# Second layer of both expert layers as one fp32 product instead of three fp16 products

## The chip, the cores and the metric

The kernel runs on one NeuronCore of a Trainium2 chip. The metric is the device time of one execution in microseconds, the median of several runs.

## What is computed

A block of a network on x of shape (8, 32, 32, 96), in fp32: a mixture of 8 experts on group-normalised x, causal attention with 6 heads on layer-normalised tokens, and a mixture of 4 experts on layer-normalised tokens, each added to its input. Both expert layers have the same form. Every token goes through every expert, and the gates of all but the top two are zero:

```python
# first expert layer: E = 8, HID = 384, 96 inputs, 96 outputs
h = jnp.einsum('bhwd,edf->bhwef', x, W1) + b1
h = jax.nn.gelu(h, approximate=False)
y = jnp.einsum('bhwef,efo->bhweo', h, W2) + b2
out = jnp.einsum('bhweo,bhwe->bhwo', y, gates)
...
# second expert layer: 4 experts of the same sizes
h = jax.nn.gelu(jnp.einsum('bsd,edh->ebsh', x, w1) + b1[:, None, None, :], approximate=False)
y = jnp.einsum('ebsh,ehd->ebsd', h, w2) + b2[:, None, None, :]
out = jnp.einsum('bse,ebsd->bsd', masked, y)
```

## The kernel before

The work is one image of 1024 tokens at a time, in 8 token tiles of 128 and 2 chunks of 512. The unit of expert work is a group, one expert on one chunk: 16 groups of the first expert layer (A) and 8 of the second (C) for each image, 192 in all. A group has two halves, and TensorE works on the first layer of one group beside the second layer of the group before:

- First layer (`first_layer`, L696): for each of 3 pieces j of 128 hidden units, three fp16 products (high and low parts of weights and inputs) with 512 columns into one of two PSUM banks `ps_u`.
- Gelu (ScalarE, `moes`, L923): the same bank is read twice, once for `hid` in fp32 (L933) and once for `hidh` in fp16 (L934).
- Low part (GpSimd, L628): `hidl` = `hid` - `hidh`, in fp16.
- Second layer (`second_layer`, L706): for each of 4 token tiles i, nine products into `ps_y`: `hidh` with the high and the low part of the second weight, then `hidl` with the high part. Tokens are the stationary operand (128x128), the 96 outputs move.
- Combination (VectorE, `combine`, L1097): `ps_y` times the gate, added to `acc`, four instructions of 128x96.

The second weights are split into `w2s` (high, low, both scaled by 64) by VectorE in the chore `split_w2`, six times, during the first image. The gates carry the factor 1/64 by a factor `WS` in `normalise` (L1082), and `gates_out` (L1092) takes it off again for the bias.

Each group has 4 slots. Everything else (maxima of the attention scores, normalisations, routing, projection) is a chore with a place in a slot, written out by hand in `schedule` (L193); each engine runs through the same list of slots in program order and waits on semaphores. A steady stage is the 16 groups A of one image, with the 72 maxima of the image before, and then the 8 groups C of the image before that. Behind it stands a softmax stage (24 steps, TensorE and ScalarE), in which no expert work is done. The images 3 to 6 are a hardware loop, the others are written out. The last 16 groups C form a tail.

`project` (L845) is a chore that the change leaves alone: 8 fp32 products for each chunk, stationary `yt` 96x128, moving `wp` 96x96.

The matmuls are all recorded at L647, a helper. `hidh` and `hidl` have two buffers each, `hid` has one. ScalarE waits before it writes `hid` until GpSimd has read it (`hl_ready`).

Of the kernel before, what the change touches and what calls it, by code (L numbers as in the profile page):

```python
# [17 lines left out]
F32 = mybir.dt.float32  # L18
F16 = mybir.dt.float16
# [7 lines left out]
P = 128  # L27
# [83 lines left out]
def spread(n, slots):  # L111
# [43 lines left out]
    "split_w2":     (None, 0),  # L155
# [37 lines left out]
def schedule(it):  # L193

    if isinstance(it, int) and it == 0:
        first = [(0, "split_w2", 0), (1, "route_a", 0, 0), (1, "route_a", 1, 0), (1, "route_a", 2, 0),
                 (2, "split_w1", 1), (3, "gates_a", 0, 0), (4, "bias_a", 0, 0), (5, "bias_a", 1, 0),
                 (6, "split_w2", 1), (7, "x_load", 0)]
        first += [(8 + 2 * n, ("split_w1", "split_w2")[n % 2], 2 + n // 2) for n in range(2 * W1_PARTS - 4)]
# [96 lines left out]
def build(nc, x, cWg, cbg, cW1, cb1, cW2, cb2, w_attn, b_attn, w_proj, b_proj,  # L296
          fWg, fbg, fW1, fb1, fW2, fb2, out):
    nc.disable_value_cache = True
    with ExitStack() as ctx:
# [9 lines left out]
        w2s = sb("w2s", [P, NE * HT, 2, D], F16)  # L309
# [34 lines left out]
        hid = sb("hid", [P, HT, CH])  # L344
        hidh = sb("hidh", [P, 2, HT, CH], F16)
        hidl = sb("hidl", [P, 2, HT, CH], F16)
# [48 lines left out]
        with nc.sbuf_tensor("w1_raw", [ONE + 1, NE * HID], F32) as w1_raw, \  # L395
                nc.sbuf_tensor("w2_raw", [P, NE * HT, D], F32) as w2_raw:
            pass
# [36 lines left out]
        w2_ready = sem("w2_ready")  # L434
# [3 lines left out]
        hl_ready = sem("hl_ready")  # L438
# [33 lines left out]
        def _(sp):  # L472
# [14 lines left out]
            def load_w2(part):  # L487
                e = 2 * part
                w, e0 = (cW2, e) if e < EA else (fW2, e - EA)
                sp.dma_start(w2_raw[:, e * HT:(e + 2) * HT, :], w[e0:e0 + 2].rearrange("e (j p) o -> p (e j) o", p=P)  # L490
                             ).then_inc(w2_loaded[part], 16)
# [75 lines left out]
        def _(pool):  # L567
# [51 lines left out]
            grp = Count(GA + GC)  # L619

            def iteration(it, moe_a, attend, moe_c):
                for up, _, phase, slots in rounds(moe_a, moe_c):
                    for slot in slots:
                        j = slot % TC
                        if up and j < HT:

                            pool.wait_ge(h_ready, grp.value(HT, j + 1))
                            g.tensor_tensor(hidl[:, grp.k % 2, j, :], hid[:, j, :], hidh[:, grp.k % 2, j, :],  # L628
                                            ALU.subtract).then_inc(hl_ready, 1)
                        for name, k, b in chores(it, phase, slot):  # L630
                            chore(name, k, b)
                    if up:
                        grp.k += 1
# [6 lines left out]
            walk(pool, [grp], iteration)  # L640

        @block.tensor
        def _(pe):
# [62 lines left out]
            def second_layer(group, i):  # L706
# [18 lines left out]
            def moes(it, moe_a, moe_c):  # L725
# [5 lines left out]
                for up, down, phase, slots in rounds(moe_a, moe_c):  # L731
                    if starts and up and up.c == 0 and up.e % 2 == 0:
                        pe.wait_ge(w1_ready, up.e // 2 + 1)
                    if starts and down and down.c == 0 and down.e % 2 == 0:
                        pe.wait_ge(w2_ready, down.e // 2 + 1)
                    if starts and phase == 1:

                        pe.wait_ge(w1_ready, W1_PARTS)
                        pe.wait_ge(w2_ready, W1_PARTS)
# [179 lines left out]
        def _(act):  # L919
# [3 lines left out]
            def moes(it, moe_a, moe_c):  # L923
                for up, _, phase, slots in rounds(moe_a, moe_c):
                    for slot in slots:
                        j = slot % TC
                        if up and j < HT:
# [96 lines left out]
        def _(dve):  # L1024
# [157 lines left out]
            def chore(name, k, b):  # L1182
# [176 lines left out]
```

## Time and profile before

| | |
|---|---|
| Median of 3 runs | 1538.88 us (1536.85 to 1539.56) |
| Span of the profiled execution | 1533.6 us |
| TensorE matmul busy | 1324.4 us (86%) |
| TensorE weight load busy | 775.0 us (51%) |
| ScalarE busy | 934.1 us (61%) |
| VectorE busy | 893.8 us (58%) |
| GpSimd busy | 716.0 us (47%) |
| Mean granted TensorE clock | 0.923 |

The profile is of one execution, whose own time is its span of 1533.6 us and what lies before and behind it; the median lies 5.3 us above the span. Matmuls are pipelined: the duration of a record is its latency, and the rate is read from one start to the next. A granted clock of 1.00 is 2.4 GHz, 0.50 is 1.2 GHz; a number between them is the mean of a stretch with both. PE is TensorE's matmul, PEld its weight load, DVE VectorE, ACT ScalarE, POOL GpSimd.

### The profile page before, as it was taken

How to read it: one execution, taken by the hardware profiler on the slowest of the kernel's cores; microseconds unless marked ns; L12 is line 12 of the kernel's file. 1: busy time of each engine (PE TensorE's matmuls, PEld its weight loads, DVE VectorE, ACT ScalarE, POOL GpSimd, SP SyncE). 2: the span in 40 equal slices, each digit the busy share in tenths (PEclk: the TensorE clock that was granted, in tenths of full speed). 3: DMA queues.
4: the chain of work that ended last, by engine and by line, in shares of the span. 5: the costliest groups of instructions: out<-in, count | busy, mean ns of one | idle time of the engine just before them, and what ended most of it. 6: DMA issues, size and time to landing. Idle time of an engine off the chain costs nothing.

```text
span 1533.6 us, 36404 instructions
## 1 busy us (share of the span) xinstructions
PE 1324.4 (86%) x12957; PEld 775.0 (51%) x12957; DVE 893.8 (58%) x2662; ACT 934.1 (61%) x1880; POOL 716.0 (47%) x656
## 2 busy tenths in 40 slices
PE   4778879888898899889898899888998898968978
PEld 1554543565536564466635565365644665333445
DVE  4865593388617784287724886177832866165362
ACT  2566537566675667656675667656676666703755
POOL 4765540467406572367605573075713665000355
PEclk9897998999999999899998999899999999956989
DMA  5000200300021000400004000210003000120100
GB/s 108 12 1 18 46 1 12 75 2 2 12 54 32 2 2 23 71 7 2 2 22 76 1 2 16 52 32 2 2 23 65 1 2 2 38 48 1 23 12 11
DMA packets 37424, 35.14 MB, mean 23 GB/s; under 512 B 26091, under 2 KB 28012, under 8 KB 37234
## 3 DMA queue, kind: packets, MB, share of 16 engines
q1 hardware_dynamic: 20594, 26.37, 8.8%
q10 hardware_dynamic: 16640, 6.29, 1.9%
q8 instruction: 113, 1.85, 0.5%
q14 instruction: 77, 0.63, 0.2%
HBM read 22.62 MB, written 9.63 MB: 21 GB/s over the span
## 4 chain that ended last, share of the span: by engine, by line
PE 30%; issue 26%; POOL 21%; DVE 13%; DMA 4%; ACT 2%; DVEq 1%; POOLq 1%; SPq 1%; ACTq 0%
POOL hidl L628 20%; PE ps_y L647 11%; PE ps_u L647 9%; PE ps_r L647 6%; DVE mpart L1156 4%; PE ps_m L647 3%; DVE xn L1138 1%; DMA ks<-qk_dram 1%; DMA qk_dram<-qk_l 1%; DVE acc L1104 1%; ACT hidh L934 1%; DVE yt L1288 1%; POOLq L608 1%; PE ps_m L666 1%; POOL rstd L609 1%
## 5 line engine op out<-in xcount | busy, mean ns | idle before, releaser
L628 POOL TENSOR_TENSOR hidl<-hid,hidh 128x512 f16<-128x512 f32 x576 | 670.7, 1185 | 686.2 <-ACT hidh L934 684.1
L933 ACT ACTIVATE hid<-ps_u 128x512 f32<-128x512 f32 x576 | 345.0, 599 | 391.8 <-PE ps_u L647 363.2
L1156 DVE TENSOR_REDUCE mpart<-ps_r 128x1 f32<-128x512 f32 (+2 forms) x576 | 297.3, 549 | 94.1 <-PE ps_r L647 79.8
L934 ACT ACTIVATE hidh<-ps_u 128x512 f16<-128x512 f32 x576 | 344.4, 598 | 0.0
L647 PEld LDWEIGHTS ps_y<-w2s,hidh 128*128 128x128 f16 x4608 | 276.4, 101 | 119.2 <-issue 24.1
L647 PE MATMUL ps_y<-w2s,hidh 128*128 128x96 f16 x4608 | 326.3, 210 | 8.0 <-DVE acc L1104 7.2
L647 PE MATMUL ps_r<-ks,qs 96*128 96x512 f16 (+2 forms) x576 | 199.9, 363 | 66.9 <-DVE mpart L1156 39.4
L647 PE MATMUL ps_y<-w2s,hidl 128*128 128x96 f16 x2304 | 231.0, 211 | 26.7 <-POOL hidl L628 26.6
L647 PE MATMUL ps_u<-xah,w1h 97*128 97x512 f16 x408 | 168.7, 414 | 29.8 <-ACT hidh L934 12.8
L965 ACT ACTIVATE probs<-ps_r 128x512 f32<-128x512 f32 (+3 forms) x352 | 152.9, 506 | 57.6 <-PE ps_r L647 57.2
L647 PE MATMUL ps_u<-xah,w1l 97*128 97x512 f16 x408 | 168.1, 412 | 0.0
L647 PE MATMUL ps_u<-xal,w1h 97*128 97x512 f16 x408 | 167.6, 411 | 0.0
L647 PEld LDWEIGHTS ps_y<-w2s,hidl 128*128 128x128 f16 x2304 | 145.0, 101 | 32.6 <-POOL hidl L628 31.7
L647 PE MATMUL ps_y<-probs,vaug 128*32 128x512 f32 (+3 forms) x1152 | 160.0, 499 | 0.1
L965 ACT ACTIVATE probs<-ps_u 128x512 f32<-128x512 f32 (+3 forms) x224 | 104.0, 517 | 27.9 <-PE ps_u L647 27.9
L1104 DVE SCALAR_TENSOR_TENSOR acc<-ps_y,gatesa,acc 128x96 f32<-128x96 f32 x448 | 109.6, 306 | 13.0 <-PE ps_y L647 11.4
L647 PEld LDWEIGHTS ps_r<-ks,qs 96*128 96x128 f16 x576 | 59.8, 104 | 111.0 <-DVE mpart L1156 68.3
L647 PE MATMUL ps_r<-qs,ks 98*128 98x512 f16 (+3 forms) x352 | 99.0, 334 | 9.1 <-DMA qs<-mtl 7.0
L647 PE MATMUL ps_r<-mask_q,identb 128*128 128x128 bf16 x384 | 90.8, 238 | 0.0
L1138 DVE TENSOR_SCALAR xn<-x,mv,rstd 128x96 f32<-128x96 f32 x128 | 83.2, 710 | 8.6 <-POOL rstd L609 8.1
L647 PEld LDWEIGHTS ps_u<-xah,w1h 97*128 97x128 f16 x408 | 42.2, 103 | 68.6 <-ACT hidh L934 27.0
L1047 DVE SCALAR_TENSOR_TENSOR qk_l<-ps_m,qk_h 96x512 f16<-96x512 f32 x32 | 22.0, 687 | 86.6 <-ACT qk_h L988 86.6
(188 smaller groups left out, 1582.0 us busy)
## 6 DMA issues: line engine op xcount, KB each, us to landing
rb<-rsum_dram SPq DMA_DIRECT2D x24, 256.0 KB, 4.2
qs<-qk_dram SPq DMA_DIRECT2D x24, 192.0 KB, 4.9
ks<-qk_dram SPq DMA_DIRECT2D x24, 192.0 KB, 4.8
xin<-in_x_dram ACTq DMA_DIRECT2D x8, 384.0 KB, 4.1
qk_dram<-qk_h SPq DMA_DIRECT2D x16, 192.0 KB, 3.1
qk_dram<-qk_l SPq DMA_DIRECT2D x16, 192.0 KB, 3.5
out_dram<-xo ACTq DMA_DIRECT2D x8, 384.0 KB, 3.0
w_raw<-in_L_conv_W_dram SPq DMA_DIRECT2D x8, 288.0 KB, 5.1
```

Of the source, the lines that this page charges most:

```text
L608: pool.drain()
L609: g.tensor_tensor(dst, dst, power[0:n, 0:dst.shape[1]], ALU.pow).then_inc(done, 1)
L628: g.tensor_tensor(hidl[:, grp.k % 2, j, :], hid[:, j, :], hidh[:, grp.k % 2, j, :], ALU.subtract).then_inc(hl_ready, 1)
L647: return nc.tensor.matmul(dst, lhsT, rhs, start=start, stop=stop, skip_group_check=True)
L666: last = nc.tensor.transpose(ps_m[0:D, P * i:P * (i + 1)], src[:, TC * c + i, :], ident[:])
L933: a.activation(hid[:, j, :], bank[:], ACT.Gelu, scale=1.0 / WS)
L934: a.activation(hidh[:, grp.k % 2, j, :], bank[:], ACT.Gelu, scale=1.0 / WS).then_inc(h_ready, 1)
L965: a.activation(probs[:, n % 3, g, 0:w], soft_bank(k)[:, 0:w], ACT.Exp, scale=float(HD) ** -0.5).then_inc(p_ready, 1)
L1047: return v.scalar_tensor_tensor(out=lo, in0=ps_m[0:D, :], scalar=scale, in1=hi, op0=ALU.mult, op1=ALU.subtract).then_inc(m_free, 1)
L1104: last = v.scalar_tensor_tensor(out=out[:, t, :], in0=ps_y[grp.k % 2][:, D * i:D * (i + 1)], scalar=r.gates[:, t, e:e + 1], in1=acc[:, t, ...
L1138: v.tensor_scalar(dst[:, t, :], src[:, t, :], mv[:, t, 0:1], rstd[:, t:t + 1], ALU.subtract, ALU.mult)
L1156: v.tensor_reduce(mpart[:, h, i, part:part + 1], ps_r[k % 3][:, 0:w], AX, ALU.max).then_inc(mx_free, 1)
```

## The change

`hid` becomes a double-buffered fp32 tile and is the second layer's only stationary operand; `hidh` and `hidl` go, with ScalarE's second Gelu, GpSimd's subtraction and the semaphore `hl_ready`. `w2s` is the fp32 weight, loaded by DMA directly, so `w2_raw` and the six `split_w2` go; TensorE waits for the DMA. The gates lose the factor 64.

```diff
-        w2s = sb("w2s", [P, NE * HT, 2, D], F16)
+        w2s = sb("w2s", [P, NE * HT, D])
...
-        hid = sb("hid", [P, HT, CH])
-        hidh = sb("hidh", [P, 2, HT, CH], F16)
-        hidl = sb("hidl", [P, 2, HT, CH], F16)
+        hid = sb("hid", [P, 2, HT, CH])
...
-                sp.dma_start(w2_raw[:, e * HT:(e + 2) * HT, :], w[e0:e0 + 2].rearrange("e (j p) o -> p (e j) o", p=P)
+                sp.dma_start(w2s[:, e * HT:(e + 2) * HT, :], w[e0:e0 + 2].rearrange("e (j p) o -> p (e j) o", p=P)
                              ).then_inc(w2_loaded[part], 16)
...
-                        if up and j < HT:
-
-                            pool.wait_ge(h_ready, grp.value(HT, j + 1))
-                            g.tensor_tensor(hidl[:, grp.k % 2, j, :], hid[:, j, :], hidh[:, grp.k % 2, j, :],
-                                            ALU.subtract).then_inc(hl_ready, 1)
...
                 for j in range(HT):
-                    for part in range(2):
-                        mm(out, hidh[:, n % 2, j, tok], w2s[:, e * HT + j, part, :], j == 0 and part == 0, False)
-                if i == 0:
-                    pe.wait_ge(hl_ready, grp.value(HT, 0))
-                for j in range(HT):
-                    last = mm(out, hidl[:, n % 2, j, tok], w2s[:, e * HT + j, 0, :], False, j == HT - 1)
+                    last = mm(out, hid[:, n % 2, j, tok], w2s[:, e * HT + j, :], j == 0, j == HT - 1)
...
                     if starts and down and down.c == 0 and down.e % 2 == 0:
-                        pe.wait_ge(w2_ready, down.e // 2 + 1)
+                        pe.wait_ge(w2_loaded[down.e // 2], 16)
...
-                            wait(act, hl_ready, grp.value(HT, j + 1 - HT))
                             bank = ps_u[(HT * grp.k + j) % 2]
-                            a.activation(hid[:, j, :], bank[:], ACT.Gelu, scale=1.0 / WS)
-                            a.activation(hidh[:, grp.k % 2, j, :], bank[:], ACT.Gelu, scale=1.0 / WS
+                            a.activation(hid[:, grp.k % 2, j, :], bank[:], ACT.Gelu, scale=1.0 / WS
                                          ).then_inc(h_ready, 1)
...
-                v.tensor_scalar(r.gt[:], ps_m[:, 0:P], WS, None, ALU.mult).then_inc(m_free, 1)
+                v.tensor_copy(r.gt[:], ps_m[:, 0:P]).then_inc(m_free, 1)
...
-                if name == "split_w2":
-                    dve.wait_ge(w2_loaded[k], 16)
-                    w = slice(2 * HT * k, 2 * HT * (k + 1))
-                    split(w2s[:, w, 0, :], w2s[:, w, 1, :], w2_raw[:, w, :], WS)
-                    dve.drain().then_inc(w2_ready, 1)
...
-                    normalise(ra, ra.gates[:, 0:TT, :], ra.prob[:], EA, 0.0, WS).then_inc(gates_a, 1)
+                    normalise(ra, ra.gates[:, 0:TT, :], ra.prob[:], EA, 0.0, 1.0).then_inc(gates_a, 1)
```

The slots of the first image lose their `split_w2` entries; the `split_w1` keep theirs, at 8, 12, 16 and 20.

The order of instructions on TensorE at the place where the turned maxima (`ps_m<-ident,mneg`) stand between two tiles of a group C, in the kernel before:

```order
1672 L647 MATMUL ps_u<-xch,w1h 128x512 [waits h_ready]
1673 L647 MATMUL ps_u<-xch,w1l 128x512
1674 L647 MATMUL ps_u<-xcl,w1h 128x512
1675 L647 MATMUL ps_y<-w2s,hidh 128x96 x6
1676 L647 MATMUL ps_y<-w2s,hidl 128x96 x3
1677 L795 MATMUL ps_m<-ident,mneg 128x128 [waits m_free,mneg_ready]
1678 L647 MATMUL ps_y<-w2s,hidh 128x96 x6
1679 L647 MATMUL ps_y<-w2s,hidl 128x96 x3
1680 L647 MATMUL ps_y<-w2s,hidh 128x96 x6
1681 L647 MATMUL ps_y<-w2s,hidl 128x96 x3
```

and the same place in the changed kernel:

```order
1330 L631 MATMUL ps_u<-xch,w1h 128x512 [waits h_ready]
1331 L631 MATMUL ps_u<-xch,w1l 128x512
1332 L631 MATMUL ps_u<-xcl,w1h 128x512
1333 L631 MATMUL ps_y<-w2s,hid 128x96 x3
1334 L775 MATMUL ps_m<-ident,mneg 128x128 [waits m_free,mneg_ready]
1335 L631 MATMUL ps_y<-w2s,hid 128x96 x6
```

Nine products of a token tile are three; nothing else moved.

ScalarE inside the groups of a steady stage, before (`ps_u` is the first layer's bank):

```order
399 L933 ACTIVATE hid<-ps_u 128x512 [waits hl_ready,y_full,up_full]
400 L934 ACTIVATE hidh<-ps_u 128x512
401 L933 ACTIVATE hid<-ps_u 128x512 [waits hl_ready,up_full]
402 L934 ACTIVATE hidh<-ps_u 128x512
403 L933 ACTIVATE hid<-ps_u 128x512 [waits hl_ready,up_full]
404 L934 ACTIVATE hidh<-ps_u 128x512
```

and in the changed kernel, two groups:

```order
199 L912 ACTIVATE hid<-ps_u 128x512 [waits y_full,up_full]
200 L912 ACTIVATE hid<-ps_u 128x512 [waits up_full] x2
201 L912 ACTIVATE hid<-ps_u 128x512 [waits y_full,up_full]
202 L912 ACTIVATE hid<-ps_u 128x512 [waits up_full] x2
```

Each group has three Gelus instead of six, and the wait for GpSimd is gone.

## Rows read from the trace of the kernel before

**Rows 1.** Page, engine totals and the chain that ended last by line

```profile
PE 1324.4 (86%) x12957; PEld 775.0 (51%) x12957; DVE 893.8 (58%) x2662; ACT 934.1 (61%) x1880; POOL 716.0 (47%) x656
...
POOL hidl L628 20%; PE ps_y L647 11%; PE ps_u L647 9%; PE ps_r L647 6%; DVE mpart L1156 4%; PE ps_m L647 3%; DVE xn L1138 1%; DMA ks<-qk_dram 1%; DMA qk_dram<-qk_l 1%; DVE acc L1104 1%; ACT hidh L934 1%; DVE yt L1288 1%; POOLq L608 1%; PE ps_m L666 1%; POOL rstd L609 1%
```

**Rows 2.** Windows: stretch, length, busy us (records) by engine, clock, DMA share, GB/s

```profile
0.00:233.20 233.20, 167.57 (x1729) 106.16 (x1730) 154.13 (x419) 116.45 (x214) 130.99 (x138) 0.89 0.15 31
...
276.30:409.50 133.20, 116.03 (x1330) 79.38 (x1329) 96.39 (x279) 81.96 (x155) 87.54 (x78) 0.96 0.11 22
...
628.20:764.90 136.70, 119.59 (x1331) 79.94 (x1332) 95.23 (x279) 84.84 (x156) 87.55 (x78) 0.94 0.12 22
764.90:806.00 41.10, 40.78 (x293) 15.24 (x289) 11.90 (x49) 31.98 (x79) 0.00 (x0) 1.00 0.08 22
...
1163.70:1297.80 134.10, 118.71 (x1294) 79.24 (x1293) 89.31 (x266) 80.82 (x153) 86.80 (x76) 0.92 0.11 19
...
1440.00:1533.60 93.60, 73.89 (x793) 48.10 (x791) 41.84 (x140) 53.92 (x102) 58.13 (x50) 0.90 0.08 19
```

**Rows 3.** Page, groups: line, engine, form, count | busy, mean ns | idle before

```profile
L628 POOL TENSOR_TENSOR hidl<-hid,hidh 128x512 f16<-128x512 f32 x576 | 670.7, 1185 | 686.2 <-ACT hidh L934 684.1
L933 ACT ACTIVATE hid<-ps_u 128x512 f32<-128x512 f32 x576 | 345.0, 599 | 391.8 <-PE ps_u L647 363.2
...
L934 ACT ACTIVATE hidh<-ps_u 128x512 f16<-128x512 f32 x576 | 344.4, 598 | 0.0
...
L647 PE MATMUL ps_y<-w2s,hidh 128*128 128x96 f16 x4608 | 326.3, 210 | 8.0 <-DVE acc L1104 7.2
...
L647 PE MATMUL ps_y<-w2s,hidl 128*128 128x96 f16 x2304 | 231.0, 211 | 26.7 <-POOL hidl L628 26.6
```

**Rows 4.** Waits of TensorE's matmuls, whole kernel: us in total, times, longest us

```profile
PE ps_r L647 <- DVE mpart L1156: 39.4, 33, 2.9
PE ps_y L647 <- POOL hidl L628: 26.6, 34, 2.4
...
PE ps_u L647 <- ACT hidh L934: 15.4, 23, 3.1
```

**Rows 5.** Timeline, TensorE at full clock: start us, us, form, count

```profile
1466.31 0.42 PE L647 MATMUL ps_y<-w2s,hidh 128*128 128x96 f16 x6
...
1466.69 0.38 PE L647 MATMUL ps_u<-xch,w1h 97*128 97x512 f16 x1
...
1464.06 1.87 PEld L647 LDWEIGHTS ps_m<-wp,yt 96*128 96x128 f32 x16
1465.82 0.38 PEld L647 LDWEIGHTS ps_y<-w2s,hidh 128*128 128x128 f16 x6
```

**Rows 6.** Timeline, TensorE at half clock

```profile
1372.14 3.49 PEld L647 LDWEIGHTS ps_m<-wp,yt 96*128 96x128 f32 x16 [1.00 <-DVE yt L1288]
1375.46 0.36 PEld L647 LDWEIGHTS ps_r<-ks,qs 96*128 96x128 f16 x2
...
633.12 0.29 PE L647 MATMUL ps_m<-wqh,xbh 97*128 97x96 f16 x1
...
634.09 0.63 PE L647 MATMUL ps_u<-xah,w1h 97*128 97x512 f16 x1
```

**Rows 7.** Timeline, a 384-column fp32 product at full clock

```profile
621.28 0.91 PE L647 MATMUL ps_m<-b2a,gta 128*128 128x384 f32 x2
622.03 0.33 PE L647 MATMUL ps_u<-qs,ks 98*128 98x384 f16 x1
```

**Rows 8.** Timeline, VectorE: two splits of first weights, first image

```profile
54.30 1.43 DVE L1032 TENSOR_SCALAR w1h<-w_raw 97x768 f16<-97x768 f32 x1
...
61.63 0.55 DVE L1032 TENSOR_SCALAR w1h<-w_raw 97x768 f16<-97x768 f32 x1
```

**Rows 9.** VectorE's groups between 40 and 75 us

```profile
L1034 DVE SCALAR_TENSOR_TENSOR w2s<-w_raw,w2s 128x576 f16<-128x576 f32 x4 | 5.4, 1344 | 0.4
L1032 DVE TENSOR_SCALAR w2s<-w_raw 128x576 f16<-128x576 f32 x4 | 4.1, 1022 | 0.5
```

More of the change, by code:

```diff
@@ L154 @@
     "split_w1":     (None, 0),
-    "split_w2":     (None, 0),
     "turn_watt":    (None, 1),
@@ L195, in schedule @@
     if isinstance(it, int) and it == 0:
-        first = [(0, "split_w2", 0), (1, "route_a", 0, 0), (1, "route_a", 1, 0), (1, "route_a", 2, 0),
+        first = [(1, "route_a", 0, 0), (1, "route_a", 1, 0), (1, "route_a", 2, 0),
                  (2, "split_w1", 1), (3, "gates_a", 0, 0), (4, "bias_a", 0, 0), (5, "bias_a", 1, 0),
-                 (6, "split_w2", 1), (7, "x_load", 0)]
-        first += [(8 + 2 * n, ("split_w1", "split_w2")[n % 2], 2 + n // 2) for n in range(2 * W1_PARTS - 4)]
+                 (7, "x_load", 0)]
+        first += [(8 + 4 * n, "split_w1", 2 + n) for n in range(W1_PARTS - 2)]
         first += [(25 + n, "turn_watt", n) for n in range(3)] + [(29 + n, "turn_wp", n) for n in range(2)]
@@ L392, in build @@
         xo = sb("xo", [P, TT, D])
-        with nc.sbuf_tensor("w1_raw", [ONE + 1, NE * HID], F32) as w1_raw, \
-                nc.sbuf_tensor("w2_raw", [P, NE * HT, D], F32) as w2_raw:
+        with nc.sbuf_tensor("w1_raw", [ONE + 1, NE * HID], F32) as w1_raw:
             pass
@@ L433, in build @@
         w1_ready = sem("w1_ready")
-        w2_ready = sem("w2_ready")
         watt_ready = sem("watt_ready")
@@ L437, in build @@
         up_full, h_ready = sem("up_full"), sem("h_ready")
-        hl_ready = sem("hl_ready")
         y_full, y_free = sem("y_full"), sem("y_free")
@@ L617, in chore @@
                     rstd(rstd2[:], mv2[:, :, 1], ln2_var, ln2_rstd, b)
-            grp = Count(GA + GC)
             def iteration(it, moe_a, attend, moe_c):
-                for up, _, phase, slots in rounds(moe_a, moe_c):
+                for _, _, phase, slots in rounds(moe_a, moe_c):
                     for slot in slots:
-                        j = slot % TC
-                        if up and j < HT:
-                            pool.wait_ge(h_ready, grp.value(HT, j + 1))
-                            g.tensor_tensor(hidl[:, grp.k % 2, j, :], hid[:, j, :], hidh[:, grp.k % 2, j, :],
-                                            ALU.subtract).then_inc(hl_ready, 1)
                         for name, k, b in chores(it, phase, slot):
                             chore(name, k, b)
-                    if up:
-                        grp.k += 1
                 for n in range(STEPS + 1):
@@ L639, in _ @@
                 chore(name, 0, Image(0, 0))
-            walk(pool, [grp], iteration)
+            walk(pool, [], iteration)
         @block.tensor
@@ L734, in moes @@
                     if starts and down and down.c == 0 and down.e % 2 == 0:
-                        pe.wait_ge(w2_ready, down.e // 2 + 1)
+                        pe.wait_ge(w2_loaded[down.e // 2], 16)
                     if starts and phase == 1:
                         pe.wait_ge(w1_ready, W1_PARTS)
-                        pe.wait_ge(w2_ready, W1_PARTS)
+                        for part in range(EA // 2, W1_PARTS):
+                            pe.wait_ge(w2_loaded[part], 16)
                         pe.wait_ge(b2c_loaded, 16 * TT)
@@ L1317, in chore @@
                     dve.drain()
-                    normalise(rc_, rc_.gates[:, 0:TT, 0:EC], rc_.ex[:, :, 0:EC], EC, 1e-9, WS).then_inc(gates_c, 1)
+                    normalise(rc_, rc_.gates[:, 0:TT, 0:EC], rc_.ex[:, :, 0:EC], EC, 1e-9, 1.0).then_inc(gates_c, 1)
                 if name == "gates_c":
```

## The prediction

> **What bounds the kernel now.** I read the engine totals and the chain of waits first, and they disagree [rows 1]: TensorE is busy 86% of the span and no other engine over 61%, yet the chain gives a fifth of the span to GpSimd's subtraction, the operation that the change takes away. The table by stage settles part of it [rows 2]. The span consists of a first stretch (0 to 233 us: prologue, first image, second image's expert layers), six steady stages of 24 groups each (133 to 139 us; three are shown), softmax stages of some 41 us between them, and a tail of 16 groups. In a steady stage TensorE is busy for all but 15 to 18 us; VectorE, ScalarE and GpSimd each have 40 us or more free. So the steady stages are set by TensorE with small gaps, and the reader is to see that GpSimd's 88 us there fit beside its 120.
>
> The list of TensorE's waits agrees [rows 4]: over the whole kernel its matmuls wait 26.6 us for the low part from GpSimd, 15.4 us for ScalarE and 39.4 us for VectorE's maxima. The 20% of the chain is therefore mostly a path that runs as long as TensorE's own, not time that TensorE stands still.
>
> **What the change costs: the products.** Of 6912 fp16 matmuls of the second layer [rows 3], three at a time become one fp32 matmul, 2304 in all. The price of three fp16 ones comes from start to start at full clock: nine begin at 1466.31 and the next form begins at 1466.69 [rows 5], so 0.38/9 = 42 ns each and 0.127 us for three. (The mean of 210 ns in rows 3 is latency; they overlap.) For fp32 there is a product of nearly the same shape in the kernel: project multiplies 96x128 stationary values by 96x96. Its 8 products leave 16 records, so each fp32 product is two loads and two matmuls. The 16 loads begin at 1464.06 and the next load at 1465.82: 1.76/16 = 110 ns per record, **0.220 us per product**. It has 96 rows instead of 128, but the same 128 columns to load, and the load is what sets this pace, see below. The excess is 0.093 us, and 2304 x 0.093 = **+215 us** at full clock.
>
> Why 110 ns: a 384-column fp32 product takes 0.75 us from its start at 621.28 to the next form at 622.03, in two records [rows 7]. It follows a stretch in which its first load was not prepared; less that one load of 0.11 us, (0.75 - 0.11)/2 = 0.32 us per record, 0.84 ns a column, so 96 columns stream in 80 ns. The missing 30 ns are the load of 128 fp32 columns, which a matmul this short cannot cover. The Trainium skill (FP8 and Floating Point Precision, TensorE Precision Notes) says that true FP32 takes four passes through the array. Four passes of 96 columns at 2.4 GHz would be an estimate of 160 ns per product and +76 us in all; the row of project, 220 ns, decides against leaving the load out.
>
> At half clock (1.2 GHz) the same two prices are 0.207 us per fp32 record (3.32/16) and 0.081 us per fp16 product of 96 columns (twelve of them between 633.12 and 634.09) [rows 6], hence 0.415 against 0.243 and an excess of 0.172, that is 0.08 us more than at full clock. The steady stages ran at a mean granted clock of 0.92 to 0.96 [rows 2], some 12% of their time at half. Half of that share I expect to go (below): 6% of 2304 products x 0.08 is **+11 us**.
>
> **What the change saves beside TensorE.** Off ScalarE go 576 Gelus of 598 ns, 344 us, and off GpSimd 576 subtractions, 671 us [rows 3]. Neither is worth its own time, because both lie beside TensorE. They are worth the gaps that they make in it. A group needs three first-layer pieces of three 512-column products and twelve second-layer products; it goes on to cost ScalarE 1.8 us instead of 3.6 and GpSimd nothing, while TensorE's part of second-layer work goes from 12 x 0.127 = 1.5 to 12 x 0.220 = 2.6 us. With every other engine relieved and TensorE 1.1 us per group slower, most of its waits have cover:
> - The 26.6 us for GpSimd go entirely, since the wait is removed, and nearly all of the 15.4 us for ScalarE [rows 4].
> - The 39.4 us for VectorE go in part. Chores on VectorE hold the maxima back, and those chores are now further apart as TensorE sees them. VectorE is also slowed now: the same split of a first weight takes 1.43 us beside GpSimd's subtractions and 0.55 us while GpSimd is idle [rows 8]. Four of the six splits of the second weights lie between 40 and 75 us, in the first image, with 4.1 + 5.4 us of VectorE [rows 9]; all six are gone.
> - What I expect to stay: the start of each stage, chains from one image to the next through DMA, and the prologue.
>
> TensorE is not busy for 100 us in the six steady stages together (17.2, 16.7, 17.1, 16.1, 17.9 and 15.4, each length less busy time; three of the rows are shown), 66 us in the first stretch and 20 us in the tail [rows 2]. I take three quarters of the first, 75 us; 20 us of the second, where the prologue and the serial chains of image 0 stay; and 8 us of the third: **-103 us**. The bounds are -42 us (only the waits for GpSimd and ScalarE) and -160 us (all steady idle time, 40 and 20 us of the others).
>
> The clock: 12% of the six stages, about 100 us, is half-clock time. Where TensorE stands still less, the clock should fall less often. I let half go, and 50 us of half-clock work take 25: **-25 us**; the bounds are 0 and -50. That the clock falls more often under fp32 cannot be excluded and is a rival.
>
> **Costed at nothing.** The loads of the second weights now land where they are used and the waits on them are on their DMAs, which end before the first group's second layer as the splits do now, with a group of first-layer work as cover; a late one costs about as long as one split, under 3 us, once. The fp32 pair of hid buffers keeps ScalarE's distance of two groups. The scale that leaves gates_out and normalise changes a constant. Softmax stages hold none of the edited work [rows 2]: GpSimd's busy time is 0 there. If all of these covers failed it would be under 5 us.
>
> **Sum.** +215 +11 -103 -25 = +98 us on the profiled span of 1533.6 us, 1631.6. The runs' median, 1538.88, is 5.3 us above that span; I carry these over and forecast **1637 us**, 6% slower. By the skill's four passes alone the same sum would be 1498.
>
> **Rivals.**
> - *The waits move instead of going.* VectorE's in-order queue still holds the maxima, so TensorE keeps all its gaps but the 42 us, and the clock gains nothing, with 12% of products at half clock (+22): 1538.9 + 215 + 22 - 42 = 1734 us. For it: VectorE's wait is the longest of TensorE's. Against: VectorE has 41 us free in a steady stage now and more later. 14%.
> - *The load hides, so it gets faster.* If in the mixed stream the load of the next half goes under the running matmul entirely, a product costs its streaming, 2 x 80 = 160 ns: 2304 x (0.160 - 0.127) = +76, less 103 and 25 and plus 11: 1498 us. The side turns where a product costs less than 0.127 + 117/2304 = 0.178 us. For it: with 384 columns to stream the second load costs nothing [rows 7]. Against: project pays 110 ns per record, sixteen in a row, with 96 columns [rows 5]. 3%. This is the case in which the skill's four passes would be the whole price.
> - *Everything idle goes.* All bounds of the savings together: 1538.9 + 215 - 160 - 50 = 1544 us, no change that matters. It needs the starts of the stages to be free of waits, and they are cold and serial now. 1%.
> - *The clock falls.* TensorE's array streams only 80 of each 110 ns. If this lets the clock stay at half in the second layer, 2304 x (0.415 - 0.127) = +664 us: above 2000 us. Against: the softmax stages, whose value products are fp32, ran at a clock of 1.00 [rows 2]. 2%.
> - *The change does not do what it says:* the order of instructions shows that it does, one matmul for three and one Gelu for two, so it has no chance of its own.
>
> **How the numbers follow.** The forecast holds 80%. Its own range is 1590 to 1695: the savings' bounds of -210 would be too kind, -165 gives 1600, and -70 gives 1695, plus 10 us below for the price of a product. With the first rival at 1734 left half in, the range is **1590 to 1735**, and it leaves out the last four cases and the edges of the first. 0.2% is about what a measurement tells from no change. Faster by more than that: 3%; within it: 1%; slower: 96%.
>
> **What would show each step.** TensorE should show 4608 records of ps_y from hid, 128x96 f32, start to start 110 ns, loads near 190 ns; if they stand 80 ns apart, the load was the wrong term. ScalarE's busy time should fall by 344 us to about 590, GpSimd's to about 45, VectorE's by some 50 to 80. Steady stages should be some 12 us longer, with TensorE idle for 3 to 8 us of each, a clock above 0.95, and softmax stages of 41 us. If TensorE's idle time stays at 17 us a stage, the first rival is right; if the clock of the steady stages falls below 0.9, the fourth. A span below 1590 us means that TensorE was less of a bound than its busy time says, since pipelined ends inflate it.

## The result: slower, but by a third of what was forecast

| | before | changed |
|---|---|---|
| Median | 1539.22 us (4 runs) | 1567.95 us (4 runs, 1565.43 to 1569.6) |
| Ratio, 95% interval | 1 | 1.0198 (1.0175 to 1.022) |
| Span of the profiled execution | 1533.6 us | 1567.9 us |
| Mean granted TensorE clock | 0.923 | 0.950 |

The change costs 29 us in the medians and 34.3 us in the spans. Forecast were 98. A ratio is always to a kernel before that ran beside, and takes the faster runs alone where the runs of one kernel lie more than 1.5% apart, which only those of `f32r` below do. The totals of the page of the changed kernel answer to [rows 1]:

```profile
PE 1465.4 (93%) x10653; PEld 1003.3 (64%) x10653; DVE 795.3 (51%) x2650; ACT 672.9 (43%) x1304; POOL 46.5 (3%) x80
...
PE 85%; DVE 5%; DMA 4%; issue 3%; ACT 2%; SPq 1%; POOL 0%; DVEq 0%; POOLq 0%; ACTq 0%
```

TensorE's busy time rose by 141 us, not 201, and its time not busy fell from 209.2 to 102.5 us, by 107, where I had said 103. GpSimd went to 46 us. ScalarE lost 261 us and not the 344 of the second Gelu's group, since the records of two Gelus in a row overlap and its total counts the overlap once. VectorE lost 98 us, more than the 50 to 80 that I gave it. The chain is now 85% TensorE.

The new groups answer to [rows 3]:

```profile
L631 PEld LDWEIGHTS ps_y<-w2s,hid 128*128 128x128 f32 x4608 | 595.6, 194 | 62.5 <-issue 3.9
L912 ACT ACTIVATE hid<-ps_u 128x512 f32<-128x512 f32 x576 | 343.0, 597 | 667.7 <-PE ps_u L631 657.6
L631 PE MATMUL ps_y<-w2s,hid 128*128 128x96 f32 x4608 | 591.3, 274 | 0.3 <-DVE acc L1082 0.3
```

There are 4608 records for 2304 products, with loads of 194 ns, as said in the forecast. The timeline gives the price (start us, duration us, form, count):

```profile
701.66 0.81 PE L631 MATMUL ps_y<-w2s,hid 128*128 128x96 f32 x6
702.30 0.60 PE L650 MATMUL ps_m<-ident,xin 128*96 128x128 f32 x4
...
710.28 0.38 PE L631 MATMUL ps_r<-ks,qs 96*128 96x512 f16 x1
710.50 1.47 PE L631 MATMUL ps_y<-w2s,hid 128*128 128x96 f32 x12
711.82 0.38 PE L631 MATMUL ps_r<-ks,qs 96*128 96x512 f16 x1
```

Three products take 0.64 us and six take 1.32, so a group's twelve take 2 x 0.64 + 1.32 = 2.60 us, 0.217 each, against the 0.220 of the forecast. The stages answer to [rows 2] (stretch, length, busy us by engine, clock):

```profile
0.00:230.60 230.60, 191.75 (x1344) 143.57 (x1344) 129.59 (x409) 72.61 (x118) 17.10 (x42) 0.93 0.14 31
272.90:414.10 141.20, 136.81 (x1042) 109.23 (x1041) 84.39 (x279) 49.60 (x83) 4.42 (x6) 0.98 0.11 20
...
639.80:783.90 144.10, 137.72 (x1042) 108.83 (x1043) 84.68 (x279) 52.02 (x84) 4.42 (x6) 0.96 0.11 20
783.90:825.10 41.20, 40.84 (x291) 15.30 (x290) 11.94 (x49) 31.98 (x79) 0.00 (x0) 1.00 0.08 24
...
1193.90:1331.80 137.90, 133.62 (x1007) 106.38 (x1006) 79.60 (x266) 48.44 (x81) 3.67 (x4) 0.99 0.10 18
1473.60:1567.90 94.30, 85.19 (x601) 66.94 (x599) 33.48 (x140) 32.62 (x54) 1.84 (x2) 0.93 0.07 18
```

The three steady stages shown are 8.0, 7.4 and 3.8 us longer than before, where some 12 were forecast, with TensorE not busy for 4 to 6 us of each, as forecast. The tail is 0.7 us longer, and the first stretch is 2.6 us shorter although it has 32 groups of dearer products. Softmax stages are as they were. The waits of TensorE's matmuls answer to [rows 4]; those for GpSimd are gone, and those for the maxima are down to 2.0 us:

```profile
PE ps_r L631 <- DMA ks<-qk_dram: 25.8, 5, 10.5
PE ps_u L631 <- issue: 12.3, 3, 4.4
PE ps_m L631 <- DVE xal L1218: 8.9, 2, 5.0
...
PE ps_u L631 <- ACT hid L912: 5.4, 5, 2.6
```

### The profile page after: what moved, and what is told of

Same layout as the page of the kernel before. It is cut to its first block, busy times and chain, and to the rows that moved or that the text cites. A ratio compares the mean times of both kernels' runs of the same rounds, so it can differ in the third digit from the quotient of the medians.

```text
span 1567.9 us, 29757 instructions
## 1 busy us (share of the span) xinstructions
PE 1465.4 (93%) x10653; PEld 1003.3 (64%) x10653; DVE 795.3 (51%) x2650; ACT 672.9 (43%) x1304; POOL 46.5 (3%) x80
## 4 chain that ended last, share of the span: by engine, by line
PE 85%; DVE 5%; DMA 4%; issue 3%; ACT 2%; SPq 1%; POOL 0%; DVEq 0%; POOLq 0%; ACTq 0%
PE ps_y L631 40%; PE ps_u L631 26%; PE ps_r L631 12%; PE ps_m L631 6%; DVE mpart L1134 2%; DMA ks<-qk_dram 2%; DMA qk_dram<-qk_l 2%; PE ps_m L650 1%; SPq L517 1%; ACT L920 0%; DVE ks L1180 0%; ACT probs L943 0%; ACT hid L912 0%; DMA qs<-mtl 0%; DVE xal L1218 0%
## 5 line engine op out<-in xcount | busy, mean ns | idle before, releaser
L631 PEld LDWEIGHTS ps_y<-w2s,hid 128*128 128x128 f32 x4608 | 595.6, 194 | 62.5 <-issue 3.9
L631 PE MATMUL ps_y<-w2s,hid 128*128 128x96 f32 x4608 | 591.3, 274 | 0.3 <-DVE acc L1082 0.3
L1134 DVE TENSOR_REDUCE mpart<-ps_r 128x1 f32<-128x512 f32 (+2 forms) x576 | 303.8, 551 | 173.4 <-PE ps_r L631 162.2
L631 PE MATMUL ps_r<-ks,qs 96*128 96x512 f16 (+2 forms) x576 | 193.7, 354 | 29.5 <-DMA ks<-qk_dram 25.8
L631 PEld LDWEIGHTS ps_r<-ks,qs 96*128 96x128 f16 x576 | 67.9, 118 | 66.8 <-DVE mpart L1134 24.3
L631 PEld LDWEIGHTS ps_r<-qs,ks 98*128 98x128 f16 x352 | 33.1, 99 | 77.5 <-ACT probs L943 53.4
L1082 DVE SCALAR_TENSOR_TENSOR acc<-ps_y,gatesc,acc 128x96 f32<-128x96 f32 x192 | 47.4, 309 | 56.7 <-PE ps_y L631 56.5
L631 PEld LDWEIGHTS ps_u<-xal,w1h 97*128 97x128 f16 x408 | 41.0, 100 | 54.5 <-issue 9.6
L631 PE MATMUL ps_u<-qs,ks 98*128 98x512 f16 (+3 forms) x224 | 65.5, 334 | 0.9 <-ACT probs L943 0.9
L631 PEld LDWEIGHTS ps_y<-probs,vaug 128*32 128x32 f32 x1152 | 30.5, 108 | 52.3 <-issue 28.2
```

Source lines behind the costliest of these rows:

```text
L631: return nc.tensor.matmul(dst, lhsT, rhs, start=start, stop=stop, skip_group_check=True)
L1082: last = v.scalar_tensor_tensor(out=out[:, t, :], in0=ps_y[grp.k % 2][:, D * i:D * (i + 1)], scalar=r.gates[:, t, e:e + 1], in1=acc[:, t, ...
L1134: v.tensor_reduce(mpart[:, h, i, part:part + 1], ps_r[k % 3][:, 0:w], AX, ALU.max).then_inc(mx_free, 1)
```

## The experiments

The first theory was that the hand-over through ScalarE and GpSimd held TensorE more than its list of waits says. The rivals: the products cost less in the mixed stream; TensorE is slow enough now to cover the waits; GpSimd's reads slowed VectorE. All times below are medians, and each ratio is to the kernel before beside it, whose medians were 1532 to 1535 us (1539 beside the changed kernel). So a few microseconds between kernels that did not run beside each other say nothing.

**Removal alone, without dearer products.** `n9` keeps nine fp16 products, one Gelu and no subtraction. It leaves out the low part of the hidden values: the last three products read the high part.

```diff
-                            a.activation(hid[:, j, :], bank[:], ACT.Gelu, scale=1.0 / WS)
                             a.activation(hidh[:, grp.k % 2, j, :], bank[:], ACT.Gelu, scale=1.0 / WS
...
-                            g.tensor_tensor(hidl[:, grp.k % 2, j, :], hid[:, j, :], hidh[:, grp.k % 2, j, :],
-                                            ALU.subtract).then_inc(hl_ready, 1)
...
-                    last = mm(out, hidl[:, n % 2, j, tok], w2s[:, e * HT + j, 0, :], False, j == HT - 1)
+                    last = mm(out, hidh[:, n % 2, j, tok], w2s[:, e * HT + j, 0, :], False, j == HT - 1)
```

> Nine fp16 products per token tile as before, but one Gelu and no subtraction (the last three products read the high part, so the low part of the hidden values is left out). Against the changed kernel only the products differ. If an fp32 product costs its 0.216 us here as in its trace, against 0.127 for three fp16 ones, it is 2304 x 0.088 = 203 us below the changed kernel, about 1365 to 1385 us. If the price of the products was what I mis-sized (excess 160 us in all, the waits as I put them), it is near 1408 us.

Measured: 1404.27 us, 0.915 (0.9115 to 0.9185), near the second number, though the price is not what differs, see below. Its page:

```profile
PE 1268.8 (90%) x12957; PEld 756.5 (54%) x12957; DVE 794.8 (57%) x2662; ACT 672.5 (48%) x1304; POOL 46.5 (3%) x80
```

This run divides the change in two along a line of spans: 1533.6, 1402.1, 1567.9 us. The removal is worth -131.5 us: TensorE's time not busy falls from 209.2 to 133.3 (-75.9), and its busy time from 1324.4 to 1268.8 (-55.6) with the same number of matmuls. The fp32 products then cost +165.8: busy +196.6, and not busy -30.8, since the slower TensorE covers waits that `n9` still has. So the second number came out by the cover, not by a cheaper product. This is one of two orders in which the change can be split; the other follows.

**The old hand-over kept under the fp32 products,** and its two parts one by one. `a_all` has both Gelus, the subtraction, and both engines waiting for it (ScalarE two groups later, since `hid` keeps its two buffers). `a_pool` is the changed kernel with a subtraction on GpSimd that reads `hid` twice; TensorE does not wait for it, ScalarE does two groups later. `a_gelu` is the changed kernel with a second Gelu.

```diff
# a_pool
+                            pool.wait_ge(h_ready, grp.value(HT, j + 1))
+                            g.tensor_tensor(hidl[:, grp.k % 2, j, :], hid[:, grp.k % 2, j, :],
+                                            hid[:, grp.k % 2, j, :], ALU.subtract).then_inc(hl_ready, 1)
...
+                            wait(act, hl_ready, grp.value(HT, j + 1 - 2 * HT))
# a_gelu
+                            a.activation(hidh[:, grp.k % 2, j, :], bank[:], ACT.Gelu, scale=1.0 / WS)
```

> The changed kernel's fp32 products inside the old hand-over: two Gelus, the subtraction, TensorE and ScalarE waiting for it (the low part is read by nobody). If the waits went because their causes were removed, they come back: about 1539 + 203 = 1740 us less half a clock gain, 1700 to 1740. If they went because a slower TensorE covers them, the time stays near the changed kernel, 1570 to 1600 us.

> The changed kernel with 576 subtractions on GpSimd again, for which TensorE does not wait. If part of the saving is VectorE's relief from GpSimd, VectorE's busy time goes back up by some 80 us and the time by 10 to 30 us. If it is not, 1568 us within 5.

> The changed kernel with a second Gelu of each bank ahead of the one that counts, its result unread. ScalarE's busy time +344 us. If the double Gelu's delay was a cause of TensorE's standing still that slower products do not cover, +10 us or more; if they cover it, within 5 us of 1568.

Measured: `a_all` 1612.97 us (1.0518, 1.0486 to 1.0549), `a_pool` 1589.73 us (1.0359, 1.0331 to 1.0388), `a_gelu` 1572.13 us (1.0246, 1.0218 to 1.0274). Against the changed kernel's 1568 that is +45, +22 and +4; by the ratios it is 49, 25 and 7. The intervals of `a_gelu` and of the changed kernel touch, so the second Gelu is not told from nothing. The page of `a_all`:

```profile
PE 1472.2 (92%) x10653; PEld 999.7 (62%) x10653; DVE 871.7 (54%) x2650; ACT 934.3 (58%) x1880; POOL 713.8 (44%) x656
```

So of the 131 us that the old hand-over costs with fp16 products, 45 are left when the products are fp32: most of it is covered by a slower TensorE, as the second theory of `a_all` says, though not all. Split in this order, by the spans 1533.6, 1607.6 and 1567.9, the fp32 products cost +74.0 and the removal gives back 39.7. The same products cost +165.8 after the removal, so neither part has a price of its own. And half of what is left comes with an operation that TensorE never waits for: in `a_pool` VectorE is busy 862.3 us instead of 795.3, some 67 of the expected 80, and ScalarE's own wait for the subtraction is 5.5 us in the list.

**Which part of the removal counts.** Four kernels made from the kernel before. All but `b_hid2` leave out the low part of the hidden values. `b_nopool` drops the subtraction alone (both Gelus stay). `b_nowait` keeps it, but TensorE reads `hidh` in its place and does not wait. `b_hid2` gives `hid` two buffers, so that ScalarE does not wait for the group before, and computes what the kernel before does. `b_free` is the last two together.

```diff
# b_nowait, b_free
-                if i == 0:
-                    pe.wait_ge(hl_ready, grp.value(HT, 0))
...
-                    last = mm(out, hidl[:, n % 2, j, tok], w2s[:, e * HT + j, 0, :], False, j == HT - 1)
+                    last = mm(out, hidh[:, n % 2, j, tok], w2s[:, e * HT + j, 0, :], False, j == HT - 1)
# b_hid2, b_free
-        hid = sb("hid", [P, HT, CH])
+        hid = sb("hid", [P, 2, HT, CH])
...
-                            wait(act, hl_ready, grp.value(HT, j + 1 - HT))
+                            wait(act, hl_ready, grp.value(HT, j + 1 - 2 * HT))
```

> The kernel before without the subtraction: the last three products read the high part (low part left out), both Gelus kept. It splits the saving of the full removal: with GpSimd as the cause of TensorE's waits about 1539 - 100 = 1440 us; with ScalarE's double Gelu as the cause, 1520 us or more.

> The kernel before with the subtraction still running and ScalarE still waiting for it, but TensorE's last three products read the high part and do not wait (low part left out). If only TensorE's own wait for the low part counts, it is 27 to 35 us faster (1505 to 1512). If GpSimd acts through ScalarE's wait or through VectorE, it stays above 1515 while the kernel without the subtraction is well below it.

> The kernel before with two buffers for the fp32 hidden values, so that ScalarE does not wait for the subtraction of the group before. Computes the same. If ScalarE's wait is what GpSimd acts through, 1430 to 1480 us; if it is VectorE, no change, 1528 to 1540.

> The kernel before with GpSimd's subtraction still reading and writing, but waited for by nobody in time: two buffers for the fp32 values, and TensorE's last three products read the high part (low part left out). If reads and hand-over add up as the run with a write-only operation says (72 and 50 us), it is 1534 - 50 = 1485. If VectorE, slowed by the reads, holds TensorE at that rate by itself, it stays at 1525 to 1535.

| | median us | ratio | 95% interval |
|---|---|---|---|
| b_nopool | 1412.76 | 0.9208 | 0.9174 to 0.9242 |
| b_nowait | 1530.83 | 0.9984 | 0.9968 to 0.9999 |
| b_hid2 | 1538.05 | 1.003 | 0.9991 to 1.0069 |
| b_free | 1528.85 | 0.9973 | 0.9943 to 1.0004 |

The subtraction is nearly everything: 122 of the 131 us, more than the 100 expected of `b_nopool`. Yet neither TensorE's wait for it (26.6 us in the list) nor ScalarE's nor both together bring more than 4 us in the medians, as long as GpSimd runs. For all three of `b_nowait`, `b_hid2` and `b_free` it was the second branch of the expectation. The waits of `b_free` show where the time went instead:

```profile
PE ps_r L647 <- DVE mpart L1154: 43.3, 34, 2.9
...
PE ps_m L666 <- DVEq L1138: 12.5, 8, 3.3
```

TensorE stands for the maxima as in [rows 4] (39.4), and 12.5 us behind another of VectorE's chores, where it stood 3.6 before.

**Length without reads.** `b_write` keeps every wait and puts in place of the subtraction an operation on 8 columns and a fill of 950, 0.20 + 0.89 = 1.09 us together instead of 1.16 (medians). Here too the low part is left out.

```diff
-                            g.tensor_tensor(hidl[:, grp.k % 2, j, :], hid[:, j, :], hidh[:, grp.k % 2, j, :],
-                                            ALU.subtract).then_inc(hl_ready, 1)
+                            g.tensor_tensor(fill[:, 0:8], epsilon[:], power[:], ALU.add)
+                            pool.drain()
+                            g.memset(fill[:, 8:], 0.0).then_inc(hl_ready, 1)
```

> The kernel before with GpSimd's subtraction replaced by an operation of about the same length that reads almost nothing and fills a tile that nobody uses; ScalarE and TensorE still wait for it, TensorE's last three products read the high part (low part left out). If GpSimd's reads slow VectorE and that is what held the kernel, it is fast, 1410 to 1440 us, with VectorE's busy time near 795 us. If the hand-over through GpSimd (the 20% of the chain) holds it, it stays at 1500 or more.

Measured: 1463.15 us, 0.9539 (0.9505 to 0.9573), between the two expectations. The waits:

```profile
PE ps_y L649 <- POOL fill L631: 35.1, 43, 2.6
...
PE ps_r L649 <- DVE mpart L1158: 7.9, 20, 0.9
```

Without GpSimd's reads the waits for the maxima fall from 39 to 8 us, and now TensorE waits for GpSimd itself, 35 us. From before to `b_write` it is -72 us, from there to `b_nopool` -50. I read this as two limits close together: while VectorE is slowed by the reads, it is the later one, and taking away the hand-over gains nothing. The 50 us are the hand-over and what the fill itself costs VectorE, which is busy 820.1 us in `b_write` against 795.2 in `b_nopool`; no run separates the two. The fill is 6% shorter than the subtraction, so the 72 us may hold some of that.

VectorE's `xn` (one SBUF tensor read) and `yt` (two) show the slowing, in the kernels before, `b_write` and `n9` in this order (count | busy us, mean ns):

```profile
L1138 DVE TENSOR_SCALAR xn<-x,mv,rstd 128x96 f32<-128x96 f32 x128 | 83.2, 710 | 8.6 <-POOL rstd L609 8.1
L1288 DVE TENSOR_TENSOR yt<-yt,rb 96x1024 f32<-96x1024 f32 x16 | 23.5, 1472 | 2.8 <-DMA rb<-rsum_dram 2.8
```

```profile
L1140 DVE TENSOR_SCALAR xn<-x,mv,rstd 128x96 f32<-128x96 f32 x128 | 51.0, 599 | 9.2 <-POOL rstd L610 8.7
L1290 DVE TENSOR_TENSOR yt<-yt,rb 96x1024 f32<-96x1024 f32 x16 | 19.4, 1216 | 2.1 <-DMA rb<-rsum_dram 2.0
```

```profile
L1129 DVE TENSOR_SCALAR xn<-x,mv,rstd 128x96 f32<-128x96 f32 x128 | 33.4, 325 | 5.5 <-POOL rstd L609 5.0
L1279 DVE TENSOR_TENSOR yt<-yt,rb 96x1024 f32<-96x1024 f32 x16 | 19.3, 1210 | 4.3 <-DMA rb<-rsum_dram 4.3
```

With two inputs an instruction is slowed by GpSimd's reads (1472 ns) and not by its fill (1216 against 1210); with one, by both (710 and 599 against 325). The Trainium skill (SBUF — State Buffer, Who interferes with whom) says that an instruction of VectorE with two SBUF inputs contends with a GpSimd instruction that reads SBUF and not with one that only writes it, and that tensor_scalar can contend through its 2-port mode. These rows agree.

**The price on each side.** `b_more` takes the low part of the weights twice, three fp16 products more per token tile; `a_more` takes the first hidden piece twice, one fp32 product more. Both sums count that part twice.

```diff
# b_more
-                    for part in range(2):
+                    for x, part in enumerate((0, 1, 1)):
# a_more
+                mm(out, hid[:, n % 2, 0, tok], w2s[:, e * HT, :], True, False)
```

> The kernel before with three more fp16 products per token tile, 2304 in all (the low part of the weights is taken twice). If TensorE sets the time, 2304 x 0.042 = 97 us slower, 1636. If the groups are held by ScalarE and GpSimd, part of it is covered: 1570 to 1600.

> The changed kernel with one more fp32 product per token tile, 768 in all (the first third is taken twice). It prices a product: 768 x 0.220 = 169 us, 1737, with TensorE as the bound. A product that costs 0.18 or less in the mixed stream gives 1706 or less.

Measured: `b_more` 1562.08 us, 1.018 (1.016 to 1.0199); `a_more` 1718.69 us, 1.1201 (1.1181 to 1.122). The same 2304 fp16 products of 42 ns that should be 97 us cost the kernel before 27 us, less than both expectations: it took 70 us of TensorE work in its stride. Its page:

```profile
PE 1387.5 (89%) x15261; PEld 859.1 (55%) x15261; DVE 895.1 (57%) x2662; ACT 934.4 (60%) x1880; POOL 715.7 (46%) x656
```

Not busy fell by 34.8 us (209.2 to 1561.9 - 1387.5 = 174.4), and busy rose by 63, not by 97. The other 34 us came back inside the busy time. The clock can account for most of them (0.944 against 0.923): half-clock time fell from 236 to 175 us, and 61 us of it become 31. How the 70 us divide is worked out further below. In the changed kernel 768 products cost 151 us, 0.196 each, between the two expectations. TensorE's busy time rose by 163.8 us, 0.213 each, near the 0.217 of the timeline, and its time not busy fell by 12.6: there TensorE is the bound, with little left to cover.

**What a record's 110 ns are.** `a_half` loads 64 tokens instead of 128 for each fp32 product.

```diff
+                q = P if grp.it is None and n < 2 else P // 2
                 for j in range(HT):
-                    last = mm(out, hid[:, n % 2, j, tok], w2s[:, e * HT + j, :], j == 0, j == HT - 1)
+                    last = mm(out[0:q], hid[:, n % 2, j, P * i:P * i + q], w2s[:, e * HT + j, :],
+                              j == 0, j == HT - 1)
```

> The changed kernel with 64 instead of 128 tokens loaded per fp32 product (after the first two groups the upper half of each token tile is left out of the second layer); the moving side is the same 96 columns. If the load sets the 110 ns of a record, a record falls to its streaming, 80 ns, and 4608 x 0.03 = 138 us go, less what TensorE then waits for others: 1440 to 1480 us. If streaming sets it, 1568 us.

Measured: 1567.26 us, 1.023 (1.0189 to 1.027), the same as the changed kernel. By the times alone streaming would be the limit. The timeline says otherwise:

```profile
706.34 0.39 PE L631 MATMUL ps_r<-ks,qs 96*128 96x512 f16 x1
706.65 1.20 PE L631 MATMUL ps_y<-w2s,hid 128*64 128x96 f32 x12
707.79 0.39 PE L631 MATMUL ps_r<-ks,qs 96*128 96x512 f16 x1
...
709.28 0.38 PE L631 MATMUL ps_u<-xal,w1h 97*128 97x512 f16 x1
709.58 0.71 PE L631 MATMUL ps_y<-w2s,hid 128*64 128x96 f32 x6
710.23 0.28 PE L631 MATMUL ps_r<-ks,qs 96*128 96x256 f16 x1
```

Twelve records and what follows them take 1.14 us, where the changed kernel takes 1.32 (710.50 to 711.82 above). Over the whole trace the median from one start to the next inside a burst is 83 ns, against 112 in the changed kernel: the load was what held the records at 110. But the product ahead of a burst is followed after 0.31 us instead of 0.22, and the burst's last record after 0.178 us instead of at the pace of the others. Each burst so pays some 0.09 us in front and 0.10 behind, while its records gain 0.03 us each. Bursts of six records, 314 of the 487 in the trace, last 0.642 us to what follows in both kernels. Gains and losses about cancel. Why the two changes between 64-column and other loads cost this is not shown here.

**Other ways.** `mix2` makes one of three hidden pieces an fp32 product and leaves GpSimd two; `b_dve` moves the subtraction to VectorE; `f32r` uses fp32's reduced form for both operands of the second layer, with VectorE copying the weights into it in the first image (those lines are left out below); `n6` leaves out the low part of the hidden values with its three products, and has one Gelu in fp16.

```diff
# mix2: pieces 0 and 1 as before, piece 2
+                        mm(out, hid[:, n % 2, j, tok], w2f[:, e * HT + j, :], j == 0, False)
# b_dve: VectorE, after the chores of each slot
+                            dve.wait_ge(h_ready, ups.value(HT, j + 1))
+                            v.tensor_tensor(hidl[:, ups.k % 2, j, :], hid[:, ups.k % 2, j, :],
+                                            hidh[:, ups.k % 2, j, :], ALU.subtract).then_inc(hl_ready, 1)
# f32r, against the changed kernel
-        w2s = sb("w2s", [P, NE * HT, D])
+        w2s = sb("w2s", [P, NE * HT, D], F32R)
...
-        hid = sb("hid", [P, 2, HT, CH])
+        hid = sb("hid", [P, 2, HT, CH], F32R)
# n6: the only products
+                        last = mm(out, hidh[:, n % 2, j, tok], w2s[:, e * HT + j, part, :],
```

> One of three hidden pieces (the last) as an fp32 product, the other two as three fp16 products each, with GpSimd's subtraction for two pieces only and two buffers for the fp32 values. Products add 768 x 0.088 = 68 us of TensorE work; the subtraction falls by a third. If each third of GpSimd's reads is worth a third of 122 us, 1534 + 68 - 41 = 1560; if the last third is where TensorE stops being held, below 1534.

> The kernel before with the subtraction on VectorE, one slot later, and two buffers for the fp32 values. Computes the same as before. 576 subtractions of some 0.6 us add 345 us to VectorE, 795 + 345 = 1140 us busy, and no port is shared with GpSimd. If VectorE has room, 1413 plus some waits, 1430 to 1480 us, faster than both kernels; if its queue delays the maxima, 1500 or more.

> The changed kernel with the hidden values and the second weights in the reduced form of fp32 (float32r), weights copied into it by VectorE. If a product leaves one record in place of two and its load is half as long, 0.11 us or less per product, 2304 x 0.105 = 240 us below the changed kernel as far as TensorE is the bound: 1340 to 1400 us. If it is two records as fp32, 1568 and a few us for the copies.

> One Gelu in fp16 and six fp16 products per token tile, the high part of the values with both parts of the weights; the low part of the values is left out. Against nine products 2304 x 0.042 = 97 us less TensorE work: 1307 us where TensorE is the bound; 1330 to 1370 if a third to a half is lost to waits and to a lower clock.

| | median us | ratio | 95% interval |
|---|---|---|---|
| mix2 | 1528.85 | 0.9963 | 0.9923 to 1.0004 |
| b_dve | 1614.59 | 1.054 | 1.0494 to 1.0587 |
| f32r | 1469.81 (of 1467 and 1473) | 0.9581 | 0.9528 to 0.9635 |
| n6 | 1362.62 | 0.8883 | 0.8841 to 0.8925 |

`mix2` cannot be told from before; the 1560 of its first branch is ruled out. `b_dve` came out slow, on its second branch, but not by the maxima. VectorE has the room in sum (1135.4 us busy of 1611.6), and TensorE waits 116.9 us for the low part behind VectorE's other work. `n6` and `f32r` beat both kernels. `n6` does it without the low part of the values, and what the reduced form costs in precision was not measured. `n6` is 11% faster than before, as expected within its wider span. None of the kernels that keep the arithmetic of the kernel before, nor `mix2`, is clearly faster.

`f32r` missed its 1340 to 1400 though its products leave one record each, 2304 in all. Its clock is the reason that its page shows (tenths by slice, `f32r` first, the changed kernel second). The four runs lie between 1467 and 1498 us, and the page is of the one of 1493:

```profile
PEclk9956789699995799856799979979999699956968
```

```profile
PEclk9989989999999999899998999999999999956989
```

A mean of 0.843 means that 31% of its span was at half clock, against 10% in the changed kernel. The runs of 1467 and 1473 us had 0.860 and 0.858, still 28%. What made the clock fall, with TensorE busy 91% of the span, was not tried.

## Why the prediction was wrong, by its steps

The sign and the picture were right: TensorE is the bound of the changed kernel, an fp32 product costs two records held by their load, and most waits went. The size was not: +98 on the span were forecast, +34.3 measured, and 1568 lies below the range.

The step that failed is the last one, the sum. It took TensorE's busy time of 1324.4 us as work: the products were to add to it in full, only the clock was to lower it, and all the standing that could be saved was to lie in the time not busy. The prediction's last sentence named this fault (busy time inflated by pipelined ends), and the sum put it at nothing. A matmul of 96 columns lasts 0.21 us in the records and is followed after 0.04, so up to 0.17 us of standing behind it does not appear.

The starts in the traces give the size. I priced each matmul by the distance from its start to the next one at full clock, the lower quartile of all pairs of the same two forms. What half clock added is counted apart, and the rest of the span is standing. It is an estimate, good to some 7 us: `b_nopool`, with the matmuls of `n9`, comes to 1161.

| us | span | work at full clock | added by half clock | standing | not busy by the page |
|---|---|---|---|---|---|
| before | 1533.6 | 1168 | 94 | 272 | 209.2 |
| n9 | 1402.1 | 1167 | 57 | 178 | 133.3 |
| a_all | 1607.6 | 1378 | 51 | 178 | 135.4 |
| changed | 1567.9 | 1372 | 61 | 135 | 102.5 |
| b_more | 1561.9 | 1260 | 67 | 235 | 174.4 |

So the kernel before stood for 272 us, 63 more than its page shows. `b_more` bears this out: its +92 us of work came with -27 of half clock and -37 of standing. The steps of the forecast against the table:

- **Price of a product, 0.220 us.** Right within 2%: 0.217 by the timeline.
- **Products, +215 and +11 for half-clock time, 226 in sum.** The table has +204, and the price explains 2304 x (0.217 - 0.127) = 207. Of the +11 little is seen: half clock adds 61 us in the changed kernel and 57 in `n9`. 22 us of the error. In busy time it is less still, 196.6 between `n9` and the changed kernel, because the longer products fill standing that the page calls busy.
- **Waits, -103.** By the measure used, time not busy, it is -106.7, which looks right. The standing that went is 137 us: 34 us of the error. How it divides depends on the order. By `n9` the removal comes first and takes 94, the products take the other 43; by `a_all` the products come first and take 94, the removal takes 43.
- **Clock, -25.** Right in its own terms: half-clock time in the six steady stages fell from 101 to 49 us. With the other stretches it is -33, 8 us of the error.

These are 64 us, the whole difference between 98 and 34. The forecast lies another 5 us off because the median was 5.3 us above the span before and is none above it in the changed kernel. Savings of 33 + 137 = 170 us lie far beyond the 128 of the sum, and near the bound of 165 that I had cut from 210. With the products at their full 226 this alone would have stayed near 1595, at the edge of the range. The result falls below 1590 because both came together. One reading was loose, without weight in the sum: VectorE was free for 37 us in the first steady stage, not for 40 or more.

**What lay behind the savings** was also not as put. I gave the waits for GpSimd and ScalarE first (-42 as the lower bound, held certain) and VectorE's relief second. With the subtraction running, both waits together are worth some 4 us (`b_free`, 9 at most by its interval); GpSimd's reads of SBUF are the first cause, some 72 us, and another 50, the hand-over and the rest of what GpSimd costs VectorE, come only behind them. That VectorE was slowed stood in the prediction with its row [rows 8], but without a term.

**The rivals.** *The waits move instead of going* needed 1734 us: wrong, the waits for the maxima all but vanished from the list. *The load hides*: wrong in the changed kernel, 0.217 us. `a_half` shows that with a short load the records stand 83 ns apart, so the mechanism was judged rightly. *Everything idle goes*, 1544 us at 1%, was nearest in time. Its savings of 210 lie as far above the 170 measured as the forecast's own 128 below them, so its nearness owes something to luck: it also had the products too dear. *The clock falls*: not with fp32, whose steady stages had 0.96 to 0.99; with the reduced form it did fall.

## What to carry to other kernels

Before a busy engine is taken as the bound, add a known amount of work to it and see how much comes back: here 97 us of small matmuls cost 27, because some 37 us of standing and 27 us of half clock went with them. The busy share of 86% hides both. Where matmuls are short, read standing from one start to the next and not from the ends. A wait in the list is worth its time only if nothing else is due just behind it, and an engine that nobody needs to wait for can still slow the one that all wait for, by what it reads from SBUF. If a low part must be made with two SBUF reads on GpSimd, price what it does to VectorE before what it does to its consumer.

## What was unexpected about the hardware

- GpSimd's subtraction with two inputs in SBUF (one fp32, one fp16) slowed VectorE's 128x96 tensor_scalar from 325 to 710 ns in the mean, and 576 of them added 99 us to VectorE's busy time (893.8 against 794.8).
- Alternating between fp32 products with a 64-column and others with a 128-column load cost TensorE some 0.09 us in front of each burst and 0.10 us behind it, as much as the shorter loads saved.
- The reduced form of fp32 leaves one record where fp32 leaves two, at the same load of 192 ns in the median, and the kernel with it ran at a mean granted clock of 0.838 to 0.860, below the profiled runs of all others here (0.916 to 0.962).
